# List entries in sets of three groups, and six shared groups held back for the final stage, in a Mamba-and-experts layer on one core

## The reference, cut to what matters

```python
def scan_layer(x):                       # L0_attn
    xc, z = split(x @ W_in.T)            # 256 + 256
    xs = silu(conv3(xc))
    dt = softplus(dt_param @ W_dt.T + b_dt) + 1e-5
    s[t] = exp(-exp(A_log) * dt[t]) * s[t-1] + B[t] * dt[t] * xs[t]   # 16 states per channel
    return ((C * s.sum(-1) + D_param * xs) @ W_out.T) * silu(z)

def expert_layer(x):                     # L0_ffn: 8 experts, 2 per token, and a shared one
    w, sel = top_k(softmax(x @ gate_w.T), 2)          # w normalised to sum 1
    y = sum over the two experts e of w_e * (gelu(x @ W1[e] + b1[e]) @ W2[e] + b2[e])
    return y + gelu(x @ sW1 + sb1) @ sW2 + sb2

x = x + layernorm(scan_layer(layernorm(x)))
x = x + layernorm(expert_layer(layernorm(x)))
```

## Time and profile before

| what | us |
|---|---|
| median of 3 runs (1260.84 to 1262.65) | 1262.3 |
| the profiled execution's own time | 1258.12 |
| its span, first to last instruction | 1256.3 |
| TensorE busy in the span | 1043.6 (83%) |
| VectorE busy | 705.6 (56%) |
| GpSimd busy | 681.0 (54%) |
| ScalarE busy | 625.3 (50%) |
| last scan ends | 692.8 |
| last matmul ends | 1242.0 |

### The profile page before, as it was taken

How to read it: one execution, slowest core, us unless ns; L and a number is a source line. 1 busy time by engine, 2 the same in 40 slices (tenths; PEclk the granted TensorE clock), 3 DMA queues, 4 the chain that set the end, 5 groups by cost and what they waited for, 6 DMA issues and landing times. The chain is left out here.

```text
span 1256.3 us, 15452 instructions
## 1 busy us (share of the span) xinstructions
PE 1043.6 (83%) x4736; PEld 832.8 (66%) x4736; DVE 705.6 (56%) x1280; ACT 625.3 (50%) x1190; POOL 681.0 (54%) x605
## 2 busy tenths in 40 slices
PE   4555578887867887797988899969999999999995
PEld 2122265664644655575777688859999999999884
DVE  1699998999988899976796442101111111111045
ACT  3784869778476586668554432212232222232234
POOL 2495967759469786578665347324343433332221
PEclk9676778898887897898999899979999999999998
DMA  5000010202002007113322589359998888887252
GB/s 180 18 28 6 34 34 18 68 1 83 2 1 84 1 18 227 42 22 110 83 96 67 172 236 208 55 150 347 337 316 266 264 276 251 262 273 227 41 176 101
DMA packets 140931, 162.68 MB, mean 129 GB/s; under 512 B 27976, under 2 KB 125984, under 8 KB 140832
## 3 DMA queue, kind: packets, MB, share of 16 engines
q1 hardware_dynamic: 124976, 142.70, 36.0%
q0 software_dynamic: 15872, 18.99, 7.7%
HBM read 135.20 MB, written 26.87 MB: 129 GB/s over the span
## 5 line engine op out<-in xcount | busy, mean ns | idle before, releaser
L1542 POOL TENSOR_TENSOR Ssum<-Ssum,S 128x512 f32<-128x512 f32 x240 | 301.5, 1270 | 105.9 <-DVE S L1162 104.7
L1014 PE MATMUL psum<-w,hT 128*128 128x256 f32 x1152 | 260.0, 384 | 4.2 <-issue 4.2
L1014 PEld LDWEIGHTS psum<-w,hT 128*128 128x128 f32 x1152 | 219.8, 193 | 34.4 <-issue 4.6
L1592 POOL DMA_INDIRECT acc_d<-y,ID x72 | 114.3, 1587 | 236.8 <-DMA acc_d<-y,ID 124.7
L1431 ACT ACTIVATE A<-dts,nea 128x512 f32<-128x512 f32 x256 | 177.3, 720 | 68.6 <-DVE S L1162 40.4
L1470 ACT ACTIVATE hT<-psum,bb 128x256 f32<-128x256 f32 x200 | 83.5, 470 | 244.7 <-PE psum L981 244.7
L981 PE MATMUL psum<-XT,w 128*128 128x256 f32 x800 | 182.8, 386 | 7.4 <-issue 6.5
L1138 DVE TENSOR_TENSOR psum<-us,psum 128x512 f32<-128x512 f32 x256 | 163.4, 682 | 31.6 <-PE psum L902 29.6
L981 PEld LDWEIGHTS psum<-XT,w 128*128 128x128 f32 x800 | 154.0, 194 | 33.9 <-issue 10.7
L1162 DVE TENSOR_TENSOR_SCAN S<-A,carry,psum 128x512 f32<-128x512 f32 x120 | 148.8, 1264 | 0.0
L1296 DVE TENSOR_TENSOR y<-bb,psum 128x256 f32<-128x256 f32 x72 | 27.0, 416 | 209.0 <-PE psum L1014 209.0
(11 more groups left out here) (149 smaller groups left out, 1314.3 us busy)
## 6 DMA issues: line engine op xcount, KB each, us to landing
w<-W SPq DMA_DIRECT2D x94, 1024.0 KB, 6.7
bb<-b SPq DMA_DIRECT2D x47, 128.0 KB, 7.8
xnb<-x SPq DMA_DIRECT2D x16, 256.0 KB, 3.0
Xr<-x SPq DMA_DIRECT2D x16, 256.0 KB, 4.6
x_d<-gb SPq DMA_DIRECT2D x8, 512.0 KB, 2.9
xn_d<-nb SPq DMA_DIRECT2D x8, 512.0 KB, 3.3
X<-x_d SPq DMA_DIRECT2D x16, 256.0 KB, 9.3
ACC<-acc_d SPq DMA_DIRECT2D x16, 256.0 KB, 5.9
```

The source lines that it names most:

```text
L1014: t = eng.matmul(bank(g)[:, 256 * k:256 * k + 256], hT[n % 2][:, f, 128 * k:128 * k + 128], w[:, f, :], start=f == 0, stop=f == 7)
L1542: eng.tensor_tensor(to, to, of, ALU.add).then_inc(nsum, 1)
L1592: eng.indirect_dma_start(acc_d, bass.IndirectOffsetOnAxis(ap=ID[:, col, 1:2].bitcast(u32), axis=0), y[n % NY][:, k, :], None, compute_op=A ...
```

## The change

It does two things. The list entries are loaded in sets, each with a semaphore of its own: the first and second round are a set each, as before, and the last round's 23 routed groups are cut into eight sets of three (the last one of two). After each set the planner may use its groups, so that the loads of later sets stand between other work in the plan. And `LATE` falls from 6 to 5: six shared groups (chunks 5, 6 and 7) are held back instead of four. With it, `calls` rises from 48 to 54.

```diff
-LATE = 6
+LATE = 5
...
+SET = 3
+SETS = [ROUTED[a:b] for a, b in zip([0] + TILES, TILES[:-1])]
+SETS += [ROUTED[a:a + SET] for a in range(TILES[-2], len(ROUTED), SET)]
+SET_OF = {group: n for n, groups in enumerate(SETS) for group in groups}
...
-        for m in range(TILES[r - 1] if r else 0, TILES[r]):
-            say("ids", m)
-        if r == NR - 1:
-            for m in range(NHALF):
-                say("ids", NT + m)
-        for _ in range(4):
-            yield
-        listed[0] = TILES[r] if r < NR - 1 else len(ROUTED)
+        for n in range(r, r + 1 if r < NR - 1 else len(SETS)):
+            say("ids", n)
+            for _ in range(4):
+                yield
+            listed[0] += len(SETS[n])
...
-                calls = 48 if listed[0] else 26
+                calls = 54 if listed[0] else 26
...
-        got_id = [sem(f"got_id{i}") for i in range(NR)]
+        got_id = [sem(f"got_id{i}") for i in range(len(SETS))]
...
-        def wait_ids(eng, r):
-
-            eng.wait_ge(got_id[r], 16 * (TILES[r] - (TILES[r - 1] if r else 0) + (NHALF if r == NR - 1 else 0)))
+        def wait_ids(eng, group):
+
+            n = SET_OF[group]
+            eng.wait_ge(got_id[n], 16 * sum(len(units(g)) for g in SETS[n]))
...
                 elif step == "ids":
-                    unit, = a
-                    r = UNIT_ROUND[unit]
-                    eng.wait_ge(select, SELECTED[NR if unit >= NT else r])
-                    if unit in (0, *TILES[:-1]):
+                    n, = a
+                    for unit in (u for group in SETS[n] for u in units(group)):
+                        r = UNIT_ROUND[unit]
+                        eng.wait_ge(select, SELECTED[NR if unit >= NT else r])
                         eng.wait_ge(tabled[r], 32 * len(ROUND[r]))
-                    row = eng.value_load(trow[0:1, unit:unit + 1], min_val=0, max_val=LROWS - (2 if unit < NT else 1))
...
+                        row = eng.value_load(trow[0:1, unit:unit + 1], min_val=0, max_val=LROWS - (2 if unit < NT else 1))
...
```

More of the change, by code:

```diff
@@ L1288, in _ @@
                         if kind != "s":
-                            wait_ids(eng, round_of(GROUPS[n]))
+                            wait_ids(eng, GROUPS[n])
                         for k in range(2):
@@ L1566, in _ @@
                     r = round_of(ROUTED[n])
-                    wait_ids(eng, r)
+                    wait_ids(eng, ROUTED[n])
                     eng.wait_ge(st_xn, 16 * ROUND_END[r])
@@ L1663, in _ @@
                 elif step == "ids":
-                    unit, = a
-                    r = UNIT_ROUND[unit]
-                    eng.wait_ge(select, SELECTED[NR if unit >= NT else r])
-                    if unit in (0, *TILES[:-1]):
+                    n, = a
+                    for unit in (u for group in SETS[n] for u in units(group)):
+                        r = UNIT_ROUND[unit]
+                        eng.wait_ge(select, SELECTED[NR if unit >= NT else r])
                         eng.wait_ge(tabled[r], 32 * len(ROUND[r]))
-                    row = eng.value_load(trow[0:1, unit:unit + 1], min_val=0, max_val=LROWS - (2 if unit < NT else 1))
-                    if unit < NT:
-                        eng.dma_start(ID[:, 2 * unit:2 * unit + 2, :], lists[:, bass.ds(row, 2), :]).then_inc(got_id[r], 16)
-                    else:
-                        eng.dma_start(ID[:, NT + unit, :], lists[:, bass.ds(row, 1), :].squeeze(1)).then_inc(got_id[r], 16)
+                        row = eng.value_load(trow[0:1, unit:unit + 1], min_val=0, max_val=LROWS - (2 if unit < NT else 1))
+                        if unit < NT:
+                            eng.dma_start(ID[:, 2 * unit:2 * unit + 2, :], lists[:, bass.ds(row, 2), :]).then_inc(got_id[n], 16)
+                        else:
+                            eng.dma_start(ID[:, NT + unit, :], lists[:, bass.ds(row, 1), :].squeeze(1)).then_inc(got_id[n], 16)
                 elif step == "fetch":
```

## The result

| | changed kernel, us | kernel before, us | ratio, 95% interval |
|---|---|---|---|
| first measurement, 11 runs each | 1254.4 (1248.2 to 1260.4) | 1264.2 (1260.8 to 1270.0) | 0.9926 (0.9908 to 0.9944) |
| profiled execution, time | 1253.4 | 1258.1 | |
| its span | 1251.5 | 1256.3 | |
| TensorE busy | 1046.5 (84%) | 1043.6 (83%) | |
| VectorE busy | 714.7 (57%) | 705.6 (56%) | |

The kernel is faster by 0.74%, some 9 us. The forecast was 17.5 us. The profiled spans differ by only 4.8 us. Against the median of before's first three runs, 1262.3, it is 7.9 us.

What follows compares the result with a forecast made beforehand. Several engines share the bound until about 700 us, then TensorE's queue and its holes. -15.1 - 0.9 + 3 - 4.5 = -17.5 us, from the median 1262.3 to 1245, range 1237 to 1257.

Steps and rivals of the forecast that it cites:

- The race: Before tile 13: TensorE misses its gathered rows at 812.6 us, they land about 806, so the margin is 6.6 us.
- The tail: Behind TensorE's last matmul: chunk 6's statistics and normalisation come earlier, one round of steps falls away, -4.5 us, bounds -4.5 and 0.
- At nothing: Counted as 0: entries spread among weight fetches, a half MB more of preset rows at the start, two stores less.
- the piece behind tile 13: From tile 13's transposition to the end of the last matmul: 402.1 us before, forecast 416.4.
- refill of 3: TensorE's drained queue behind tile 13: 0.89 us copying rows out of PSUM plus 2 for late rows, +3 us.
- a bubble of 2: TensorE waits for tile 14's rows, whose gather stands behind tile 12's scatter on GpSimd: 2 us, bounds 0 and 6.
- The rivals: Partly filled hole 0.17; nothing gained, last table write binding, 0.07; slower by the scan stage 0.08; more, 1238 us, within 0.68.
- partly filled hole: Tile 13's rows slip by 12 us: a hole of 5 and slow start of 2.5 return, 1252 us; chance 0.17.
- -15.1: At tile 13: TensorE's 12.55 us wait for gathered rows and the 2.54 us slow start behind it both go.
- its clock at 0: Behind the refill's wait for tile 14's rows, TensorE's matmuls are not slowed: 0 us, bounds 0 and 1.8.
- the scan stage, 0: Two more routed groups beside the scans, 12.8 us on GpSimd, hidden in its idle time: 0, bounds -4 and +8.
- -0.9: Behind the buffers' widening: two shared groups replace routed ones on TensorE, 2 x (14.25 - 13.82) = 0.9 us less.

Runs made afterwards that it cites:

- first batch: Each against the kernel before: changed kernel again 0.9895; sets alone 0.9884; groups held back alone (54 steps) 1.0167; changed kernel at 48 steps a chunk 1.0101.
- second: Against the kernel before: changed kernel 0.995; with epsilon addition moved to GpSimd 0.9882; sets alone with that move 0.9898; changed kernel with scatters one step later 0.9968.
- third: Against the kernel before: that kernel itself 0.9999; changed kernel 0.9861; sets alone 0.986; changed kernel with the epsilon addition moved to GpSimd 0.9809.
- fourth: With epsilon addition on GpSimd, against the kernel before: changed kernel 0.9823; also scatters one step later 0.9793; sets alone 0.9806. Kernel before, one more run: 1260.6 us.
- fifth: Changed kernel unedited, 1258.0 us against 1264.6, ratio 0.9954; the kernel before once more on the same chip, one run, 1263.9 us.
- the shift: Each scatter after the scan stage one step later: on the changed kernel 1258.9 us, 0.9968; with the epsilon addition on GpSimd too, 1235.8 us, 0.9793 of before.
- the kernels with the addition moved: Addition of epsilon to the variances moved from VectorE to GpSimd: changed kernel 1248.5, 1238.2 and 1239.0 us; sets alone 1251.0 and 1237.4 us.

## Why the prediction was right and wrong

**Right: why the rows were late, and how the change brings them forward.** The hole is gone and with it the slow start. The race was told to 1 us: rows first wanted 76.9 us behind the last logits' transposition, measured 77.8 and 77.9 in the changed kernel's two profiles without the stall; entries from 57.3 us behind it, measured 57.5 in the first profile and 58.1 and 57.2 in those two. That last match is partly luck: the last table write came 52.9 us behind the transposition (790.32 with 737.39) against the 51.5 forecast, and the first entry 4.5 us behind it, where I had 5.9. The tail lost 4.49 us of 4.5. "At nothing" held for the entries among the weight fetches; for the preset rows the late start of some profiles leaves it open.

**Luck: the piece behind tile 13.** It was forecast at 416.4 with its refill of 3, and is 416.35 in the first profile and in all others of such a kernel with the stall. But my 3 was a pause of 0.89 and a bubble of 2 for late rows, and those profiles have no such bubble: the stall has let the rows catch up, and the pauses are 1.58 and 0.83. Without the stall, which is what I forecast, it is 421.2.

**The rivals.** None of them came about: the median lies near the 1252 of "partly filled hole", but TensorE waits for no rows at tile 13.

**Wrong: the step "-15.1" was booked in full, as if only the late rows made the time at the hole of 12.55 us.** Before the hole lies a stretch of the run in which an execution may stall for 10 to 15 us. The kernel before pays 2 to 4 us of it (108.2 against 104.1 to 106.4), since TensorE arrives late at rows that are later still. The changed kernel has no wait left there to absorb it and pays 10 to 14 (87.9, 89.9 and 91.6 against 77.8), of which 4.9 come back behind tile 13, where the wait for rows and its slow part fall away (416.35 against 421.2): 5 to 9 net. By batches:

| batch | stall in the profiles | before, us | changed kernel, ratio |
|---|---|---|---|
| first measurement | changed kernel yes, before no | 1264.2 | 0.9926 (0.9908 to 0.9944) |
| first batch | none of 4 | 1259.9 | 0.9895 (0.9869 to 0.9921) |
| second | all 4 | 1263.9 | 0.995 (0.9919 to 0.998) |
| third | none of 4 | 1261.4 | 0.9861 (0.9838 to 0.9884) |
| fourth | none of 4 | 1263.2 | (not run) |
| fifth | both | 1264.6 | 0.9954 (0.9937 to 0.9972) |

By the medians the gain without the stall is 13.6 and 13.5 us (1259.9 - 1246.3 and 1261.4 - 1247.8; by the ratios 13.2 and 17.5), and with it 6.4 to 9.8. So the stall explains 4 to 7 us of what is missing from 17.5, and some 4 by the medians are missing without it too. Of those the profiles show the two terms below, the refill (4.9 over the forecast) and the scan stage (2.3). I had no way to see the stall in the one profile of before, which has none; but I could have seen that a hole also hides what is late ahead of it, and put a bound on that.

**Mis-sized: the refill, +3.** Its bubble was put at 2 us with bounds of 0 and 6, and its clock at 0 with bounds of 0 and 1.8. Without the stall, in two profiles of the changed kernel, it measured 7.9 instead of 3: the 3 that are there with the stall too, a wait of 2.95 us, a slow part behind it of 1.7, and 0.2 in smaller pieces. I had also taken the order wrong. I had TensorE want tile 14's rows 16.1 us behind tile 13's (828.7 - 812.6); the plan turns group 14 9.2 us behind it and tile 15 17.8 (825.28, 834.44 and 843.09 in the first profile), group 14's gather goes out ahead of the scatters that wait, and it is tile 15's that stands behind them. I had taken 0 for the clock, and the rule of the Trainium skill that I had weighed ("TensorE: Matmul & The Clock Gate", "What's actually happening") gave 2 us more: the wait of 2.95 us agrees with the rule and my row didn't, while behind the wait of 2.01 us in the fourth batch the part took the usual 7.07. The true case lies within my bounds each time, and for a wait of this length I chose the wrong one. The cause was named rightly (a gather behind scatters that wait for landings): with it away the wait is gone, which was worth 0.5 to 1.1 us where the wait was 2.01 and 0.28 us. On the changed kernel itself, with its 2.95, the shift ran only with the stall.

**Mis-sized: the scan stage, 0.** From the second first-scan of chunk 0 to the last scan's end the changed order takes 645.5 to 649.1 us in seven profiles (with 54 steps), and the kernels with four groups held back 643.0 to 647.4 in six (the additions left where they were). The spread of 3 to 4 us within each comes from earlier chunks, in kernels of both kinds, and isn't the change; the means are 2.3 us apart, 647.3 and 645.0. That part lies in chunks 5 to 7 (2.4 us more together in the first batch), and what is known of it points to the swap of two shared groups for two routed tiles in chunk 7. In the first profile it is given back at once, as the transposition behind the last logits follows the last scan after 40.4 us instead of 43.0; that is why the table says -0.3. In the fourth batch the difference to the sets alone is 2.1 us there.

**And the half that did nothing.** I had six groups held back worth 2.4 us: -0.9 and -4.5 against the +3. They measure 2.0 us on the other side in the two profiles of the fourth batch, which are of the kernels with the addition moved, and by the ratios of the first, third and fourth batch six groups and four are not to be told apart (0.9895 and 0.9884, 0.9861 and 0.986, 0.9823 and 0.9806). The tail's gain is real, and paid back in the refill and the scans, which the sets alone don't have: with seven groups to run while the routing is done they never drain TensorE's queue, and their piece behind tile 13 takes 399.65 us with no pause in it.

**What stays open.** The stall's cause. The rows show when it comes (while GpSimd writes the lists), who has it (TensorE, ScalarE and VectorE; of the sync queue some of these profiles show issues of 0.00 and 0.02 us there that usually take 0.38), who has not (GpSimd), and that in each of the five batches all profiles agree on it, while in the first measurement the changed kernel's has it and before's has not. None of my kernels took it away or brought it on. Each kernel of a batch has one profile, so how many of the other executions have the stall is not known. The lowest ratio measured is one of the fourth batch, with the addition on GpSimd and the scatters a step later: 0.9793 of before, not told apart from the 0.9806 and 0.9809 of the kernels next to it.

## What to carry to other kernels

A wait that you remove was also a cushion: whatever came late ahead of it was nearly free (2 to 4 us here), and is paid once the wait is gone (10 to 14 there, 5 to 9 net). Before you book a hole as gain, look at more than one execution and ask what else varies in the stretch ahead of it. And when a change has two parts, run each alone: here one brought all of it, the other alone lost 1.7%, and together they were no better than the first.

## What the runs showed of the hardware

- An addition of four numbers a partition on VectorE took 4.45 us instead of 0.23, until three sums of GpSimd in a row had ended. Moved to GpSimd, where 32 of them take 8.0 us in all (20.1 on VectorE in the first profile), it shortened the changed kernel's scan stage by 4.1 and 6.9 us in the two batches that have both.
- For 10 to 15 us more than usual three engines run late while GpSimd goes on, in some batches and not in others, with no wait that the profile could name ("issue", "remote").
- A wait of 2.95 us on TensorE was followed by 32 matmuls in 8.76 us, one of 2.01 us by 32 in 7.07. The granted clock was 0.83 of full speed from 837 to 847 us in the first case, a mixture of the two levels (1.2 and 2.4 GHz), and 1.00 from 827 to 837 in the second.
- A scatter to memory that adds landed late enough to hold up the next by 7.50 us while weights were loaded, and a gather that another engine wanted stood behind both.
